# Expert layer: routing moved into the second attention, a DRAM region per expert, results scattered straight to the output

## The reference

```python
def _L1_ffn_ref(x, W1, b1, W2, b2, Wg, bg):     # 16 experts, 192 -> 192 -> 192
    t = x.reshape(-1, Dx)                        # 2864 tokens
    logits = t @ Wg.T + bg
    idx = jnp.argmax(logits, axis=-1)            # one expert per token
    out = jnp.zeros_like(t)
    for e in range(W1.shape[0]):
        mask = (idx == e).astype(t.dtype)[:, None]
        h = jax.nn.gelu(t @ W1[e].T + b1[e], approximate=False)
        y = h @ W2[e].T + b2[e]
        out = out + mask * y
    return out.reshape(Bx, Nx, Dx)
...
h = h + _L1_ffn_ref(_layernorm(h, axis=-1), ...)
```

## Time and profile before

| | us |
|---|---|
| median of 3 runs | 1578.75 |
| lowest, highest | 1565.89, 1581.03 |
| the profiled execution | 1580.39 |
| its span in the profile | 1578.5 |
| second attention, first maximum to last addition to `resid` | 1040.9 to 1392.8 |
| last logits; routing done; first product on a tile | 1410.5; 1428.7; 1464.4 |
| last product on a tile; last addition to `resid` | 1534.9; 1574.6 |

### The profile page before, as it was taken

How to read it: one execution, slowest core, us unless ns; L and a number is a source line. 1 busy time by engine, 2 the same in 40 slices (tenths; PEclk the granted TensorE clock), 3 DMA queues, 4 the chain that set the end, 5 groups by cost and what they waited for, 6 DMA issues and landing times.

```text
span 1578.5 us, 39532 instructions
## 1 busy us (share of the span) xinstructions
PE 1161.5 (74%) x16019; PEld 875.2 (55%) x16021; DVE 1127.1 (71%) x2120; ACT 1003.3 (64%) x977; POOL 868.2 (55%) x963
## 2 busy tenths in 40 slices
PE   0547778887778888778877598479999999850880
PEld 0335555665555656556655488356666666630880
DVE  6979899898889998898988658524666666532342
ACT  0129999999999999999999667322333333310440
POOL 3619788878888788888788824400111111116235
PEclk9889999999999999999999999757999999855895
DMA  7300000000000000000000000000000000051334
GB/s 200 103 0 2 2 2 2 2 2 2 2 2 2 2 2 2 2 2 2 2 2 2 1 1 0 1 0 1 2 3 2 3 3 2 2 123 54 97 95 120
DMA packets 39013, 33.65 MB, mean 21 GB/s; under 512 B 5411, under 2 KB 37352, under 8 KB 38856
## 3 DMA queue, kind: packets, MB, share of 16 engines
q1 hardware_dynamic: 28782, 22.44, 5.1%
q10 hardware_dynamic: 7516, 4.53, 1.0%
q0 software_dynamic: 2560, 4.41, 1.0%
HBM read 18.84 MB, written 11.89 MB: 19 GB/s over the span
## 4 chain that ended last, share of the span: by engine, by line
issue 30%; PE 23%; POOL 20%; ACT 13%; DVE 10%; DMA 2%; POOLq 1%; DVEq 1%; SPq 0%; ACTq 0%
POOL work L420 11%; ACT work L821 10%; PE psum L1593 8%; PE psum L1546 5%; PE psum L1547 5%; ACT pt_region L810 3%; DVE work L420 2%; POOL norm_wide L594 2%; PE psum L1620 2%; POOL xs_dram L742 1%; POOL work L761 1%; DVE work L1041 1%; PE psum L1606 1%; DMA work<-in_x 1%; POOL trstd L696 1%
## 5 line engine op out<-in xcount | busy, mean ns | idle before, releaser
L821 ACT ACTIVATE work<-work 128x2864 f32<-128x2864 f32 (+1 forms) x272 | 688.6, 2577 | 33.5 <-DVE work L420 32.8
L420 POOL TENSOR_TENSOR work<-shared 128x1253 f32<-128x1253 f32 (+1 forms) x272 | 611.9, 2261 | 133.3 <-PE psum L1593 125.7
L1593 PE MATMUL psum<-work,ws_place 128*32 128x179 f32 x8640 | 396.3, 325 | 167.6 <-ACT work L821 167.5
L420 DVE TENSOR_TENSOR work<-psum,shared 128x1611 f32<-128x1611 f32 (+3 forms) x288 | 486.5, 1722 | 0.6
L1593 PEld LDWEIGHTS psum<-work,ws_place 128*32 128x32 f32 x8640 | 261.3, 112 | 275.4 <-ACT work L821 216.2
L675 POOL TENSOR_TENSOR tsum<-tstats 128x4 f32<-128x4 f32 x16 | 3.6, 226 | 363.3 <-DVE tstats L1261 363.3
L1762 PE MATMUL psum<-shared 32*64 32x179 f32 (+1 forms) x1728 | 143.1, 369 | 8.2 <-DVE shared L1349 8.2
L1127 DVE SCALAR_TENSOR_TENSOR p_sb<-psum,bs_col,s_top 128x358 f32<-128x358 f32 x144 | 82.2, 571 | 43.9 <-PE psum L1606 30.7
L1762 PEld LDWEIGHTS psum<-shared 32*64 32x64 f32 (+1 forms) x1728 | 81.6, 160 | 57.0 <-issue 36.7
L1355 DVE TENSOR_SCALAR pt_region<-pt_region 128x1074 uint32<-128x1074 uint32 x48 | 34.6, 721 | 89.4 <-ACT pt_region L881 89.4
L810 ACT ACTIVATE pt_region<-psum,bs_neg 128x512 f32<-128x512 f32 x144 | 95.2, 662 | 1.6 <-PE psum L1606 1.5
(11 more groups left out here) (311 smaller groups left out, 2024.9 us busy)
## 6 DMA issues: line engine op xcount, KB each, us to landing
xs_dram<-zeros SPq DMA_DIRECT2D x1, 3648.0 KB, 13.3
pt_region<-xs_dram SPq DMA_DIRECT2D x38, 96.0 KB, 2.0
ys_dram<-shared ACTq DMA_DIRECT2D x38, 96.0 KB, 1.6
work<-in_x SPq DMA_DIRECT2D x4, 768.0 KB, 11.1
pt_region<-scores_dram SPq DMA_DIRECT2D x4, 512.0 KB, 5.7
pt_region<-in_L_ffn_W1T SPq DMA_DIRECT2D x1, 1536.0 KB
work<-in_L_ffn_W2T SPq DMA_DIRECT2D x1, 1536.0 KB
out<-resid SPq DMA_DIRECT2D x16, 96.0 KB
```

Source lines behind the costliest of these rows:

```text
L420: ins = eng.tensor_tensor(dst[:, a * KEEP:e * KEEP].rearrange("p (u s) -> p u s", s=KEEP), k[:, h * KP:h * KP + KEEP].unsqueeze(1).to_broa ...
L821: act.activation(a, a, ACT.Tanh).then_inc(tanh_done, 1)
L1593: ins = pe.matmul(bank_s[p % 2][32 * quad:32 * quad + 32, at:at + KEEP], ws_place[:, j, :], arg_slot(n)[:, u * KEEP:(u + 1) * KEEP], start ...
```

## The change

**The region per expert.** `xs_dram` gets 49024 rows of 386 numbers (75.7 MB): expert e owns rows from e x CAP on, CAP = 2944, so that a token's slot needs no count of other experts' tokens. A row holds the normalised token (192), a 1 for the bias, the token's number, and the residual (192). The fill at the start writes all rows by 24 DMAs on SP's queue, with a number out of the output's range as the token number, so that rows without a token are dropped at the end.

**Routing per sequence.** Turn b of the second attention gets `choose(b-4)` and `place(b-5)` on DVE, `prefix_mm(b-5)` on PE (five products of 16 columns in bfloat16), `stage_resid(b-3)` on ACT, and `stage_index(b-3)` and `send_rows(b-5)` (two indirect DMAs) on POOL. `norm4` writes straight into one of four staging buffers, and its copy (L1394) is gone. The expert weights are loaded during the second attention. What is left behind the loop is the plan of the tiles, 14 small DVE instructions.

**Tiles.** The loops are written out. SP loads the even tiles and ACT the odd ones, 128 x 386 numbers each, into a ring of eight buffers, each load behind a register read of the tile's first row and a wait until the buffer's last result has landed. ACT copies the turned tile, applies GELU and now copies the second matrix; DVE copies the turned hidden tile and the first matrix, and adds the result to the residual part of the tile; POOL scatters that sum straight to `out` by the token numbers. The 24 gathers, the additions and the stores behind the tiles are gone.

```diff
+CAP = -(-B * KEEP // 128) * 128
+XS_ROWS = EXPERTS * CAP + (XT - CAP // 128) * 128
+RW = 2 * D + 2
+RING, TILE_RING = 4, 8
...
+        def load_tile(eng, i):
+            row = eng.value_load(owner_i[i:i + 1, 1:2], min_val=0, max_val=XS_ROWS - 128)
+            if i >= TILE_RING:
+                eng.wait_ge(y_sent[i % TILE_RING], 16 * (i // TILE_RING))
+            eng.dma_start(xs[i % TILE_RING], xs_dram[bass.ds(row, 128), :]).then_inc(xs_loaded[i % TILE_RING], 16)
...
+            for lo in range(0, XS_ROWS, 2048):
+                n = min(2048, XS_ROWS - lo) // 128
+                sp.dma_start(xs_dram[lo:lo + 128 * n, :].rearrange("(j p) d -> p j d", p=128),
+                             pad_row[:, :].unsqueeze(1).to_broadcast([128, n, RW])).then_inc(e_zeroed, 16)
...
+            sp.wait_ge(tiles_ready, 1)
+            for n in range(RING):
+                sp.wait_ge(sent[n], 32 * B // RING)
+            for i in range(0, XT, 2):
+                load_tile(sp, i)
...
+            for b in range(B + 5):
+                if real(b - 3):
+                    stage_index(b - 3)
+                if real(b - 5):
+                    send_rows(b - 5)
+                if b % 2 == 0 and real(b // 2 - 1, B // 2):
+                    pair_norms(b // 2 - 1, 1)
...
+            for i in range(XT):
+                pool.wait_ge(ey_ready, i + 1)
+                pool.indirect_dma_start(rows_out, bass.IndirectOffsetOnAxis(ap=xs[i % TILE_RING][:, D + 1:D + 2].bitcast(U32), axis=0),
+                                        ey[i % 4][:, :], None, bounds_check=B * KEEP - 1,
+                                        oob_is_err=False).then_inc(y_sent[i % TILE_RING], 16)
...
+            load_tile(act, 1)
+            load_tile(act, 3)
+            for i in range(XT + 2):
                 if real(i, XT):
                     act.wait_ge(exT_psum, i + 1)
                     need(act, eh_psum, i - 1)
-                    act.activation(x[0][:, :], bank_k[par % 2][:, 0:128], ACT.Copy)
-                    act.activation(x[1][0:DB, :], bank_k[par % 2][0:DB, 128:256], ACT.Copy).then_inc(exT_ready, 1)
+                    act.activation(exT[i % 2][:, :], bank_k[i % 2][:, 0:WIDE], ACT.Copy).then_inc(exT_ready, 1)
+                if i % 2 and real(i + 2, XT) and i > 1:
+                    load_tile(act, i + 2)
                 if real(i - 1, XT):
...
+                if real(i - 2, XT):
+                    j = i - 2
...
+                    e = act.value_load(owner_i[j:j + 1, 0:1], min_val=0, max_val=EXPERTS - 1)
+                    need(act, ey_psum, j - 1)
+                    act.activation(tile_w[1][j % 2], ew2[:, :, bass.ds(e * D, D)], ACT.Copy).then_inc(w2_fetched, 1)
...
+                if real(b - 4) or real(b - 5):
+                    gate_move(b - 4)
                 if real(b - 4):
-                    gate_move(b - 4)
+                    choose(b - 4)
+                if real(b - 5):
+                    place(b - 5)
...
+            for i in range(XT + 4):
+                if real(i - 2, XT):
+                    dve.wait_ge(ehT_psum, i - 1)
+                    dve.tensor_copy(ehT[i % 2][:, :], bank_pt[i % 2][:, 0:WIDE]).then_inc(ehT_ready, 1)
                 if real(i + 1, XT):
+                    fetch(i + 1)
+                if real(i - 4, XT):
+                    j = i - 4
+                    dve.wait_ge(ey_psum, j + 1)
+                    if j >= 4:
+                        dve.wait_ge(y_sent[(j - 4) % TILE_RING], 16 * ((j - 4) // TILE_RING + 1))
+                    dve.tensor_tensor(ey[j % 4][:, :], xs[j % TILE_RING][:, D + 2:RW], out_banks[j % 2][:, 0:D],
+                                      ALU.add).then_inc(ey_ready, 1)
...
+            def prefix_mm(b):
+                pe.wait_ge(hot_ready, b + 1)
+                pe.wait_ge(gate_out, b + 1)
+                h, out = hot[b % 2], prefix_cols.rearrange("p (n e) -> p n e", n=3)
+                pe.matmul(out[:, 0, :], lower16[:, :], h[:, 0, :], start=True, stop=True)
...
```

More of the change, by code:

```diff
@@ L178, in build @@
-        ew2 = [work[:, 2 * EXPERTS * D:3 * EXPERTS * D], work[0:DB + 1, 3 * EXPERTS * D:4 * EXPERTS * D]]
-        xn4 = xn3
-        KE = 2 * B * EXPERTS
+        BLOCK = EXPERTS * D
+        ew1, ew2 = (work[:, 2 * n * BLOCK:2 * (n + 1) * BLOCK].rearrange("p (r c) -> p r c", r=2) for n in range(2))
+        FREE1 = 2 * PT1 + ROUNDS * WIDE
+        stage = [part.rearrange("p (t c) -> p t c", t=2) for part in
+                 (w1_store[:, 0:2 * RW], w1_store[:, 2 * RW:4 * RW], w2_store[:, 0:2 * RW], pt_region[:, FREE1:FREE1 + 2 * RW])]
@@ L192, in build @@
[L192 to L195 removed]
+        iota_p = sb("iota_p", [128, 1])
+        ones_e = sb("ones_e", [128, EXPERTS])
+        cap_e = sb("cap_e", [128, EXPERTS])
+        carry = sb("carry", [128, EXPERTS])
@@ L379, in build @@
         ey_ready = sem("ey_ready")
-        ys_stored = [sem(f"ys_stored{n}") for n in range(4)]
         pair_stats = sem("pair_stats")
@@ L649, in _ @@
             pool.memset(ctx1[:, :, :], 0.0)
+            pool.memset(ew2[:, 1, :], 0.0).then_inc(ew_blank, 1)
+            for n in range(2):
+                pool.memset(eh[n][:, :], 0.0)
             for n in range(2):
@@ L758, in _ @@
-            for m in range(B // 2):
-                need(pool, summed, 2 * m - 6)
-                for k, rows in ((4 * m, TA), (4 * m + 2, TA), (4 * m + 1, 2 * TB)):
-                    pool.indirect_dma_start(xn4[0:rows, k, :], None, ys_dram[:, :],
-                                            bass.IndirectOffsetOnAxis(ap=slots_of(k)[0:rows, :], axis=0)).then_inc(back[m % 4], 16)
+            pool.wait_ge(f_added, B)
+            for n in range(RING):
+                pool.memset(stage[n][:, :, D:D + 1], 1.0)
@@ L765, in _ @@
+            for n in range(TILE_RING):
+                pool.wait_ge(y_sent[n], 16 * len(range(n, XT, TILE_RING)))
         @block.scalar
@@ L896, in ctx1T_move, with stage_resid @@
                                ACT.Copy).then_inc(ctx1T_ready, 1)
+            def stage_resid(c):
+                act.wait_ge(added1, c + 1)
+                if c == 0:
+                    act.wait_ge(f_added, B)
+                if c >= RING:
+                    act.wait_ge(sent[c % RING], 32 * (c // RING))
+                act.activation(stage[c % RING][:, :, D + 2:RW], resid[:, c + 1, :, :], ACT.Copy).then_inc(staged_in, 1)
             def gxT_move(b):
@@ L1502, in expert_step @@
-                if real(i - 2, XT):
-                    dve.tensor_copy(ehT[two][1][0:DB, :], bank_pt[two][0:DB, 128:256]).then_inc(ehT_ready, 1)
-            dve.wait_ge(e_loaded, 16 * 9)
-            fetch(tile_w[0][0], ew1, expert_of(0)).then_inc(w1_fetched, 1)
-            staged(dve, expert_step, (1, 4), XT, 4)
-            for b in range(B):
-                m = b // 2
-                dve.wait_ge(back[m % 4], 48 * (m // 4 + 1))
-                for t, rows in TILES:
-                    if t and b % 2:
-                        dve.wait_ge(parted[m % 2], 16 * (m // 2 + 1))
-                    r = resid[0:rows, b + 1, t, :]
-                    ins = dve.tensor_tensor(r, r, xn4[0:rows, 2 * b + t, :], ALU.add)
-                ins.then_inc(summed, 1)
+                    fetch(i + 1)
@@ L1933, in expert_step @@
                     need(pe, eh_ready, i - 2)
-                    product(bank_s[1 - two][:, 0:D], [x[:, :] for x in exT[1 - two]], tile_w[0][1 - two]).then_inc(eh_psum, 1)
+                    product(bank_s[n][:, 0:D], halves(exT[n]), [tile_w[0][n][:, r, :] for r in range(2)]).then_inc(eh_psum, 1)
                 if real(i - 2, XT):
@@ L1942, in expert_step @@
                     need(pe, ey_ready, i - 4)
-                    product(out_banks[1 - two][:, 0:D], [x[:, :] for x in ehT[1 - two]], tile_w[1][1 - two]).then_inc(ey_psum, 1)
-            staged(pe, expert_step, (0, 8), XT, 4)
+                    product(out_banks[n][:, 0:D], halves(ehT[n]), [tile_w[1][n][:, r, :] for r in range(2)]).then_inc(ey_psum, 1)
 _TURNED = ["L0_attn_Wq", "L0_attn_Wk", "L0_attn_Wv", "L0_attn_Wo", "L0_ffn_W1", "L0_ffn_W2",
```

410 lines of the change are left out of this document (190 added, 220 removed).

## The result

| us | before | changed |
|---|---|---|
| median (lowest to highest, runs) | 1579.89 (1565.89 to 1582.20, 4) | **1535.20** (1530.95 to 1537.99, 4) |
| span of the profiled execution | 1578.5 | 1532.8 |
| first product on a tile; end of the last | 1464.4; 1534.9 | 1434.8; 1521.5 |

The account below looks back on a forecast made before the run. PE bounds the second attention and the tile loop, serial chains the last turns and the end. First product -34.3, loop +15.2, tail -39.7 sum to -58.8: span 1519.7, time 1521.6 us, range 1500 to 1550.

Parts of the forecast that it names:

- The fill: Start: writing 75.7 MB instead of 3.7 is covered by the first attention, cost 0; rival that it is not, chance 0.04.
- the ring in the tile loop: Tile loop: a load waits for an earlier tile's result to land, 8T = 4T + 8.0 to 8.6; T taken as 2.15 us.
- DVE's thirteen instructions: Second-attention turns: routing on DVE, 2.1 us more than two copies, fits its room, cost 0; rival not hidden, chance 0.10.
- POOL's sends: Second-attention turns: thirty of 32 sends fit in POOL's idle time; only the last two follow the last slots.
- The rule of the Trainium skill on a `tensor_load`: Tile loop: a floor of about 600 ns per register read would make the sum 6 to 13 us later.
- a delay of POOL's descriptors by DVE's copies: Tile loop: by the skill's rule each send waits about 0.4 us more, T + 0.1, 4 us in all.
- The tail: Behind the last product: 3.9 us instead of 43.6, so -39.7 us, ends -41 and -37.
- send 0.3 + 2.6, end about 0.6: Behind the last tile's addition: the last scatter's start and landing, then the program's end, within the 3.9 us.
- PE in the turns: Second attention: five small products add 0.5 us in each of eleven turns, +5.5 us, ends 4 and 10.
- The chain to the first product: Last turns, routing, sends and load: first product at 1430.1 instead of 1464.4, -34.3 us with the turns' 5.5 included.
- The loop, +15.2 forecast: First to last tile product: 85.7 us instead of 70.5 at 2.15 us a tile, ends +2.3 and +28.
- A slower clock: Tile loop: PE's waits let its clock fall to 1.2 GHz, about 1560 us; chance 0.03.

Follow-up runs that it names:

- the run with the waits on SP: Changed kernel with SP instead of POOL making the last waits for the scatters' landings; median 1532.33 us, ratio to before 0.9762.
- pair with the extra products: Kernel before and changed kernel, each with four unread PE products before the wait for maxima in every second-attention turn; medians 1553.67 and 1505.96 us.
- the early slots: Changed kernel with four unread products a turn, twelve buffers, loads and last waits on SP, sequence 14's slots one turn earlier; median 1488.24 us.
- twelve buffers: Changed kernel with twelve tile buffers in the ring instead of eight, loads still over both queues; median 1510.20 us, ratio to before 0.9650.
- the five products doubled: Changed kernel with the five token-counting products made twice in each turn; one run, 1562.69 us.
- DVE's copies added: Changed kernel with eight more small linked DVE copies behind each choice of experts; one run, 1602.69 us.

## Why the prediction was right or wrong

**Right in direction and mechanism.** What bounds what was read rightly: PE in the attention, a chain in the last turns, the ring in the tile loop (its interval 2.19 us from the first tile's turning to the last's, against 2.15), and the gathers, additions and stores behind the last product gone. The fill, DVE's thirteen instructions and POOL's sends cost nothing that the profiles can tell, each with a run or a row behind it. The rule of the Trainium skill on a `tensor_load` ("DMA: Bandwidth & Descriptors", Latency and other measured facts) was rightly not taken: the reads in the loop take 0.27 to 0.31 us, and what made the loop longer than forecast was the ring. Nor is a delay of POOL's descriptors by DVE's copies to be seen, as "SBUF — State Buffer" of the Trainium skill (SBUF: two separate sides, the trap by which DVE blocks DMA) would have it: all 38 scatters take POOL 0.98 to 1.01 us each, and the 0.8 us until one starts are the same in the last turns (1422.3 to 1423.1), where DVE makes no wide copy.

**The tail, -39.7 forecast, -32.3 measured.** The step "send 0.3 + 2.6, end about 0.6" failed, and it is over half of the error of 13.1 us. It left out the drain of POOL's program, 5.8 us, because in the trace of before that drain lay under other work, and POOL's scatters at 1.29 us, which fall behind additions 0.7 to 0.9 us apart. Moving the waits took 1.6 us off; the drain remained.

**PE in the turns, +5.5 forecast, +0.8 at a steady clock.** I priced five small products by weight loads of 0.073 us and added a wait; the trace shows 0.1 to 0.2 us, and doubling them cost 0.1. What the profile shows instead are three turns of 3.1 us more each, at 1.2 GHz, and a start of the attention that was quicker than before by 3.5. In the run with the waits on SP, whose program is the same up to the last scatter, it fell once and elsewhere, so this is the clock's scatter from one execution to the next; whether the change makes falls more frequent is open. By chance the wrong term hid the noise.

**The chain to the first product.** Without the turns' term I had -39.8. The pair with the extra products shows -35.1 (-35.3 less the 1.0 by which its attention started earlier, and with the 0.8 of the turns taken off), but 2.6 us of the difference are its clock in front of the last addition. From the last addition on I had 31.8 us to the first product (1392.8 to 1424.6), and both pairs show it in the changed kernel: 33.6 and 33.8, where the kernel before needs 71.6 and 71.5. So the chain fell short by 2 us. The mis-sized steps: the last send starts 3.7 us behind the last slots, not 1.6, since four sends stand there and not two (shown by the early slots), and from its landing to the first product it is 4.1 us where I had 3.0, with 1.0 to 1.5 to the load's issue instead of 0.5. The last slots came 1.2 us sooner than reckoned, 22.2 us behind the last addition instead of 23.4. These were only read. The landing was right by luck: the text says 2.3 to 2.9 us, its sum has 3.8 (1417.8 to 1421.6), and 3.6 was measured.

**The loop, +15.2 forecast, +16.2 measured, +19.7 in the pair with the extra products.** The ring was the limit, shown by twelve buffers. Its sum is 9.2 us for four tiles where I had 8.0 to 8.6: the scatter lands 2.7 to 3.2 us after its start, and POOL starts it 0.8 us after the addition, not 0.3. Kernels with a ring of eight and loads on both queues needed 86.7 to 90.5 us in seven profiles. The four longest, 88.1 to 90.5, each hold one stretch of 3.4 us at 1.2 GHz inside the loop, the other three, 86.7 to 88.0, none. At half the clock such a stretch costs at most 1.7 us, so it is part of the spread and not shown to be all of it.

**The rivals.** A slower clock was given 0.03, and only for the tile loop. In the changed kernel's profile it was at 1.2 GHz there only for the first 2.8 us, but with the ring of eight it fell inside the loop in four other profiles. The place where it cost most was the second attention, whose PE stands idle 1.0 us in a turn. The forecast read the clock of 1.00 in that stage of one execution as a property of the kernel.

## What to carry to other kernels

Before costing a tail, look at what every engine does behind its last useful instruction, the drain of POOL's program too, and ask whether the work that hides it is still there. Where a ring waits for a landing, count the round trip and widen the ring before moving queues: the engine with the largest wait may only be where the wait is shown. And where PE waits about 1 us in each turn at the full clock, one profile does not tell its time; take the noise out of both kernels, by filling that wait, before comparing them, and then check the granted clock of both stage by stage all the same.

## What the runs showed of the hardware

PE's clock fell to 1.2 GHz in turns in which PE was busy 36.98 of 40 us. With 1.0 us of idle time at one place of a turn and 0.5 at another it fell in none to three of the thirteen turns between 1090 and 1355 us, mostly in other turns from profile to profile; with 1.2 and 0.5 in every second turn; with 2.5 in every turn; with the 1.0 filled in none of them, in four kernels' profiles (in one of these it fell later, at 1361), and with 0.9 left in front of eight products in none either, at 37.13 busy. Each fall cost 3.1 us in a stretch of 6.8 us; one of 13.7 cost 6.6 with the five products doubled and 5.2 with DVE's copies added. The scatter from run to run goes with it: of seven runs of the kernel before three took 1559 to 1565 us at a mean clock of 0.920 to 0.922, and four 1577 to 1581 at 0.909 to 0.912. POOL's drain at the end of its program ended 5.8 us after its own start (1526.8) where all scatters had landed, and 5.8 us after the last scatter's end (1513.5) where it started before them; in the kernel before, over queued gathers, it ended 4.5 us after the last one's end. Writing 75.7 MB at up to 357 GB/s beside the first attention left ACT, the bound there, at 180 of 200 busy us (181.6 before).
